# Who copies the transposed rows out of PSUM, and how row statistics are joined, in a macaron block on one core

## The reference

```
x = x + 0.5 * ffn(layernorm(x))
x = x + attn(layernorm(x))
x = x + 0.5 * ffn(layernorm(x))

# ffn: a mixture of experts, E = 16, width 128, and 2 shared experts
logits = x @ router_w.T ; scores = sigmoid(logits) ; s = scores + bias
# 4 groups of 4 experts; the 2 groups with the best top-2 sums; of them the top 4 experts
tw = scores of the four / their sum * 2.5
h = x @ gate_w[e] ; u = x @ up_w[e] ; y = (silu(h) * u) @ down_w[e]
routed = sum over e of y * weight[e] ; shared: silu(x @ sh_gate) * (x @ sh_up) @ sh_down
# attn: 32 heads of 4, no softmax, a group norm per head over all positions, output projection
```

## Time and profile before

| | |
|---|---|
| median of 3 runs | 740.83 us (739.88 to 741.75) |
| profiled execution, its own time | 739.06 us |
| its span in the trace | 737.3 us |
| PE busy | 677.0 us (92%) |
| DVE busy | 601.3 us (82%) |
| POOL busy | 433.6 us (59%) |
| ACT busy | 399.6 us (54%) |
| chain that ended last | PE 45%, DVE 28%, issue 15%, POOL 6%, ACT 3%, DMA 2% |

### The profile page before, as it was taken

The page is one execution under the profiler, slowest core; times in us unless marked ns, Lnnn a source line. Parts: engine busy times, 40 slices in busy tenths (PEclk is TensorE's granted clock), DMA queues, the critical chain, the costliest instruction groups (busy, mean ns, idle before and its releaser), DMA issues.

```text
span 737.3 us, 12023 instructions
## 1 busy us (share of the span) xinstructions
PE 677.0 (92%) x3116; PEld 539.6 (73%) x3116; DVE 601.3 (82%) x1571; ACT 399.6 (54%) x784; POOL 433.6 (59%) x373
## 2 busy tenths in 40 slices
PE   2497999999999998999988999889998999999997
PEld 2376878787877866678766787667776878787885
DVE  2889797969799797997978979879799797969664
ACT  2464556565666544656445564455654556565553
POOL 4565657575756645656555474554646657575664
PEclk9699999999999999999999999999999999999999
DMA  6550614060604105033060150500605014050600
GB/s 179 179 203 1 231 35 196 3 228 0 230 2 156 76 23 210 0 93 137 2 228 1 39 191 15 206 26 16 228 15 201 30 52 193 17 229 14 231 15 15
DMA packets 30789, 76.37 MB, mean 104 GB/s; under 512 B 3968, under 2 KB 12688, under 8 KB 30736
## 3 DMA queue, kind: packets, MB, share of 16 engines
q1 hardware_dynamic: 30736, 75.81, 28.7%
HBM read 73.18 MB, written 2.62 MB: 103 GB/s over the span
## 4 chain that ended last, share of the span: by engine, by line
PE 45%; DVE 28%; issue 15%; POOL 6%; ACT 3%; DMA 2%; DVEq 1%; POOLq 0%; SPq 0%; ACTq 0%
DVE T L961 9%; POOL A_lo L323 6%; PE gateP L413 6%; PE gateP L415 5%; PE gateP L414 5%; PE upP L413 4%; PE upP L415 4%; PE yP L413 4%; PE upP L414 4%; PE yP L415 4%; PE yP L414 4%; DVE A L983 3%; ACT gateP L664 1%; PE prepP L444 1%; DVE wsum L851 1%
## 5 line engine op out<-in xcount | busy, mean ns | idle before, releaser
L323 POOL TENSOR_TENSOR A_lo<-A,A_hi 128x512 fp32r<-128x512 f32 x288 | 372.6, 1300 | 197.1 <-ACT A_hi L681 196.6
L681 ACT CAST A_hi<-A 128x512 fp32r<-128x512 f32 x288 | 177.2, 615 | 121.6 <-DVE A L983 117.0
L664 ACT ACTIVATE gateP<-gateP 128x512 f32<-128x512 f32 x256 | 148.8, 581 | 137.9 <-PE gateP L415 136.4
L961 DVE TENSOR_TENSOR T<-gateP,CB 128x512 f32<-128x512 f32 x256 | 175.2, 684 | 55.2 <-ACT gateP L664 49.4
L983 DVE TENSOR_TENSOR A<-upP,T 128x512 f32<-128x512 f32 x256 | 177.0, 692 | 9.2
L413 PE MATMUL gateP<-XT_hi,W_hi 128*128 128x512 f32 x288 | 125.9, 437 | 17.5 <-DVE T L961 17.0
L413 PE MATMUL upP<-XT_hi,W_hi 128*128 128x512 f32 x288 | 115.1, 400 | 0.0
L415 PE MATMUL gateP<-XT_lo,W_hi 128*128 128x512 f32 x288 | 114.0, 396 | 0.0
L414 PE MATMUL gateP<-XT_hi,W_lo 128*128 128x512 f32 x288 | 113.6, 394 | 0.0
L415 PE MATMUL upP<-XT_lo,W_hi 128*128 128x512 f32 x288 | 113.6, 394 | 0.0
L413 PE MATMUL yP<-A_hi,W_hi 128*128 128x512 f32 x288 | 113.0, 392 | 0.6 <-POOL A_lo L323 0.6
(11 more groups left out here) (169 smaller groups left out, 677.6 us busy)
## 6 DMA issues: line engine op xcount, KB each, us to landing
CB<-combT SPq DMA_DIRECT2D x128, 512.0 KB, 6.2
out_dram<-X SPq DMA_DIRECT2D x8, 256.0 KB, 2.0
X<-in_L_attn_x_dram SPq DMA_DIRECT2D x3, 512.0 KB, 6.2
W_in<-in_L_ffn_gate_w_dram SPq DMA_DIRECT2D x4, 256.0 KB, 5.1
W_in<-in_L_ffn_up_w_dram SPq DMA_DIRECT2D x4, 256.0 KB, 5.1
W_in<-in_L_ffn_down_w_dram SPq DMA_DIRECT2D x4, 256.0 KB, 5.3
X<-in_L_attn_x_dram SPq DMA_DIRECT2D x2, 256.0 KB, 3.6
combT<-CT SPq DMA_DIRECT2D x16, 32.0 KB, 1.8
```

What stands on the lines that cost most here:

```text
L323: pool.tensor_tensor(A_lo[:, slot, :], A[:, slot, :], A_hi[:, slot, :].bitcast(F32), ALU.subtract).then_inc(low_done, 1)
L664: act.activation(dst, gateP[u % 2][:, :], ACT.Silu).then_inc(silu_done, 1)
L681: act.copy(A_hi[:, v % SLOTS, :], A[:, v % SLOTS, :]).then_inc(high_done, 1)
L961: dve.tensor_tensor(T[:, u % TS, :], gateP[u % 2][:, :], CB[:, e, :], ALU.mult).then_inc(gate_weighted, 1)
```

## The change

Three things are done together.

1. ACT reads `prepP` twice at w = 0, first with a cast to `XT_hi`, then as a plain copy to `XT`. DVE's copy (`next_full`) is gone, and so is the wait of ACT for it. `next_low` (POOL) and `logits` (PE) move from w = 1 to w = 2; the parts of `route` from w = 2 to 9 to w = 3 to 10; the transpose of the weights and their copy by ACT from w = 11 and 12 to 12 and 13; `route_silu` from w = 3 to 4. The residual stays at w = 7.
2. `bn_stats` moves from w = 12 to w = 11, and the seven operations behind it give way to four `bn_aggr`, one a tile, at w = 12 (`whole_stats`). In the places where attention work stands at u = 11 and u = 29, `bn_stats` comes ahead of it.
3. POOL adds epsilon and changes the sign of the mean, two operations of 128 x 4 ahead of the power.

```diff
-        parts = sb("parts", [P, 5, TILES])
+        mv = sb("mv", [P, TILES, 2])
+        eps_t = sb("eps_t", [P, TILES])
+        minus = sb("minus", [P, TILES])
...
             def step_rstd(t):
-                pool.wait_ge(stats_seq, 4 * (t + 1))
+                pool.wait_ge(stats_seq, 2 * (t + 1))
+                pool.tensor_tensor(vareps[:, :], mv[:, :, 1], eps_t[:, :], ALU.add).then_inc(rstd_ready, 1)
+                pool.tensor_tensor(nmean[:, :], mv[:, :, 0], minus[:, :], ALU.mult).then_inc(rstd_ready, 1)
+                pool.wait_ge(rstd_ready, 4 * t + 2)
                 pool.tensor_tensor(rstd[:, :], vareps[:, :], half[:, 0:TILES],
                                    ALU.pow).then_inc(rstd_ready, 1)
-                pool.wait_ge(rstd_ready, 2 * t + 1)
+                pool.wait_ge(rstd_ready, 4 * t + 3)
                 pool.tensor_tensor(shift[:, :], nmean[:, :], rstd[:, :], ALU.mult).then_inc(rstd_ready, 1)
             def next_low(t, q):
-                pool.wait_ge(xt_hi_ready, t + 1)
+                pool.wait_ge(xt_ready, t + 1)
...
-                    if w == (7 if early else 1) and not (last and s == 1):
+                    if w == (7 if early else 2) and not (last and s == 1):
                         next_low(2 * p + s + 1, (s + 1) % 2)
...
-                        if w == (7 if early else 1):
+                        if w == (7 if early else 2):
                             logits(t0 + s + 1)
-                        if w == (16 if early else 11):
+                        if w == (16 if early else 12):
                             transpose_weights(t0 + s + 1)
...
             def next_high(t, q):
-                act.wait_ge(xt_ready, t + 1)
-                act.copy(XT_hi[:, q, :], XT[:, :]).then_inc(xt_hi_ready, 1)
+                act.wait_ge(xt_done, t + 1)
+                act.copy(XT_hi[:, q, :], prepP[:, :])
+                if not (isinstance(t, int) and t == 0):
+                    act.wait_ge(xt_lo_ready, t)
+                act.copy(XT[:, :], prepP[:, :]).then_inc(xt_ready, 1)
...
-                        if w == (9 if early else 3):
+                        if w == (9 if early else 4):
                             route_silu(t0 + s + 1)
-                        if w == (17 if early else 12):
+                        if w == (17 if early else 13):
                             copy_weights(t0 + s + 1)
...
-                merge_stats(stats_seq, 4 * t, bst, nmean[:, :], vareps[:, :], parts)
-
-            def next_full(t):
-                dve.wait_ge(xt_done, t + 1)
-                if not (isinstance(t, int) and t == 0):
-                    dve.wait_ge(xt_lo_ready, t)
-                dve.tensor_copy(XT[:, :], prepP[:, :]).then_inc(xt_ready, 1)
+            def whole_stats():
+                for j in range(TILES):
+                    ins = dve.bn_aggr(mv[:, j, :], bst[:, j, :])
+                ins.then_inc(stats_seq, 1)
...
+                    if w == 12 and not last:
+                        dve.wait_ge(stats_seq, 2 * (t0 + s + 2) + 1)
...
                     if not (last and s == 1):
-                        at = 6 if early else 0
-                        if w == at:
-                            next_full(t0 + s + 1)
-                        if at + 2 <= w < at + 10:
-                            route(t0 + s + 1, w - at - 2)
+                        at = 8 if early else 3
+                        if at <= w < at + 8:
+                            route(t0 + s + 1, w - at)
                     if w == 12 and not last:
+                        whole_stats()
+                    if w == 11 and not last:
                         dve.wait_ge(mul_done, n + u + 1)
                         stats(t0 + s + 2, 2 * ((p + 1) % BATCH) + s)
```

More of the change, by code:

```diff
@@ L221, in macaron_kernel @@
         stats_seq, rstd_ready, xn_ready = sem("stats_seq"), sem("rstd_ready"), sem("xn_ready")
-        xt_done, xt_hi_ready, xt_lo_ready = sem("xt_done"), sem("xt_hi_ready"), sem("xt_lo_ready")
+        xt_done, xt_lo_ready = sem("xt_done"), sem("xt_lo_ready")
         xt_ready = sem("xt_ready")
@@ L599, in normalise @@
             def normalise(t, blk, part):
-                act.wait_ge(rstd_ready, 2 * (t + 1))
+                act.wait_ge(rstd_ready, 4 * (t + 1))
                 for j in range(part * TILES // 2, (part + 1) * TILES // 2):
@@ L968, in pair @@
                     early = first and s == 0
-                    if w in ((13, 14) if early else (7, 8)) and not (last and s == 1):
-                        dve.wait_ge(route_seq, ROUTE_OPS * (t0 + s + 1) + (21 if w in (7, 13) else 22))
+                    if w == 12 and not last:
+                        dve.wait_ge(stats_seq, 2 * (t0 + s + 2) + 1)
+                    if w in ((13, 14) if early else (8, 9)) and not (last and s == 1):
+                        dve.wait_ge(route_seq, ROUTE_OPS * (t0 + s + 1) + (21 if w in (8, 13) else 22))
                     dve.wait_ge(silu_done, n + u + 1)
@@ L989, in pair @@
                         stats(1, 1)
+                        dve.wait_ge(stats_seq, 3)
+                        whole_stats()
                     if not (last and s == 1):
-                        at = 6 if early else 0
-                        if w == at:
-                            next_full(t0 + s + 1)
-                        if at + 2 <= w < at + 10:
-                            route(t0 + s + 1, w - at - 2)
+                        at = 8 if early else 3
+                        if at <= w < at + 8:
+                            route(t0 + s + 1, w - at)
                     if w == 12 and not last:
+                        whole_stats()
+                    if w == 11 and not last:
                         dve.wait_ge(mul_done, n + u + 1)
@@ L1003, in pair @@
                         attention_stage(u, p - ATT0)
+            dve.memset(eps_t[:, :], EPS)
+            dve.memset(minus[:, :], -1.0)
             dve.memset(comb[:, :], 0.0)
@@ L1007, in _ @@
             stats(0, 0)
-            next_full(0)
+            dve.wait_ge(stats_seq, 1)
+            whole_stats()
             dve.wait_ge(router_in, 32)
             dve.wait_ge(const_seq, CONSTS)
-            dve.wait_ge(xt_hi_ready, 1)
+            dve.wait_ge(xt_ready, 1)
             dve.tensor_tensor(XT_lo[:, 0, :], XT[:, :], XT_hi[:, 0, :].bitcast(F32),
```

## The result

The changed kernel takes **754.13 us** (median of 6 runs, 752.33 to 756.85); the kernel before took 740.03 on the same chip (6 runs). The ratio is 1.0189, 95% interval 1.0173 to 1.0205. The forecast was 731.0, with a range from 724.5 to 739: wrong in sign. The profiled span grew from 737.3 to 751.5.

A forecast was written before the change was run, and what follows sets the result against it. PE was taken to bound plain steps, with gains only from its idle time in attention steps and step 0. Terms -3.6 - 6.0 + 0 + 0.7 - 1.0 + 0.1 = -9.8 off median 740.83 gave 731.0 us, range 724.5 to 739.

The forecast's parts named there:

- signs of being right: No logits wait at loop heads, w = 7 gate matmul on time, first attention steps near 45, second 47.2, plain 39.7 to 39.9.
- signs of being wrong: Second attention steps above 49, ACT's Silu waiting behind both copies, `bn_aggr` as long as `bn_stats`, or the w = 7 stall remaining.
- Plain steps: Steps 1, 2, 3, 12, 13: old stall stays, DVE slightly overfull at w = 11; +0.13 each, +0.7 in all.
- port rule: A DVE operation with two SBUF inputs shares a port with GpSimd; whichever starts first holds it for the whole instruction.
- rival B: Second attention steps: `wsel`, `wsum + 1e-20` and `comb` each blocked by an `A_lo`; +4 a step, total 747; chance 0.09.
- Second attention steps: Steps 5, 7, 9, 11: +0.9 `bn_stats`, +1.1 one routing block, -2.0 two operations freed; 0, between -1 and +3 each.
- Loop heads: Steps 6, 8, 10: PE's wait for `XT` shrinks, 1.1 saved plus 0.1 for a restart; -1.2 each, -3.6 in all.
- w = 3 to 16 of first attention steps: Steps 4, 6, 8, 10: stalls at w = 7 and 15 go, `s_row` comes late; -1.5 each, -6.0 in all.
- Step 0 and start: Step 0: `comb` 1.0 earlier, PE's wait 2.94 to 1.9, -1.0; start: logits 0.4 later, +0.1.
- Prices: Costs of added work: four `bn_aggr` about 0.4 a step; ACT's copies and POOL's two operations nothing.

## Why the prediction was wrong

The step that failed is the move of the routing by one unit, which the prediction put at nothing in the plain steps and at the loop heads and at a gain in the second attention steps; it costs 27.7. Of the 24 us between the forecast and the profile 7.5 lie in the plain steps, 9.2 behind the loop heads and 6.3 in the second attention steps. Its signs of being right name the length of a plain step (39.7 to 39.9; it is 41.0), none of its signs of being wrong does.

- *Plain steps*, forecast +0.7 in all, bounds -1 to +4: **+8.2**. It read "one unit later the same string begins and ends one unit later, so this stall stays". The string is not the same: w = 7 holds the residual, ahead of the routing part, and part 4, with its two-input `masked`, came to stand behind it and beside POOL's `A_lo`, 1.36 instead of 0.22. I costed the removed and added work of w = 11 and never laid the moved parts beside what stood in their new units. Both views were there: the order of the instructions and POOL's `A_lo`, one in every unit. And I had put the port rule in front of rival B only, for the attention steps, though `A_lo` runs in plain steps as well.
- *Second attention steps*, forecast 0: **+6.3** in all. Rival B had one of the two mechanisms, `wsum` and `comb` held up by the pile, and PE's wait for `comb` is 1.51 there; the other is `masked` again, 1.59 at w = 10. I gave rival B 0.09 and +4 a step; measured were +1.6, with the statistics moving the other way: with them alone at the old places these steps fell by 1.35.
- *Loop heads*, forecast -1.2 a head and with the -1.5 of the next point -2.7 a step: steps 6, 8 and 10 came out **+0.3** each. The wait for `XT` went as said, and with the copies alone it was worth 1.7 a head, more than my 1.2. But I took the 3 us on issue for a constant. They follow the DMA traffic, and the edit moved the traffic. Behind the wait of 1.86 at 298.95 the granted clock was 0.60 (298.95 to 304.00), mostly 1.2 GHz; with DVE unrolled, without the wait, it was 1.00 in the same place. But the clock is not what the step lost: behind the head of step 8 PE waited longer, 2.02, and had 1.00, and that step takes 48.2 against 48.3 and 48.4 of steps 6 and 10. Step 8 has later waits instead (0.94 at w = 7, 0.53 for `comb`, 0.46 for `s_row`), which step 6 does not have. The table by stretch of the changed kernel behind the heads of steps 6 and 8:

```profile
298.95:304.00 5.05, 5.04 (x18) 4.36 (x19) 4.86 (x17) 1.72 (x3) 3.74 (x3) 0.60 0.00 0
396.01:401.06 5.05, 4.87 (x25) 4.16 (x26) 4.86 (x17) 3.02 (x6) 3.79 (x3) 1.00 0.00 0
```

and of the changed kernel with DVE unrolled:

```profile
299.00:304.00 5.00, 5.00 (x25) 4.19 (x25) 4.76 (x17) 3.28 (x8) 4.09 (x5) 1.00 0.00 0
```

- *w = 3 to 16 of first attention steps*, forecast -1.5 each: step 4, which has no head, gained **1.3**. Right in size there, and mostly for the reasons given: the waits of 1.44 at w = 7 and 0.52 at w = 15 are gone, the one for `s_row` is 0.44 instead of the 1.0 put in; a wait of 0.54 for `comb` came on top. In step 8 the one at w = 7 is still 0.94.
- *Step 0 and start*, forecast -0.9: **0**, but traces of the same code differ there by up to 1.4, so one trace of each kernel could not show it. But PE's wait for `comb`, which was to fall from 2.94 to 1.9, is 3.42, and it is 3.42 with copies and aggregate at the old places too: `comb` did not come earlier against PE.
- *Prices*: four `bn_aggr` 0.37 (forecast 0.4); ACT's copies hidden; POOL's two operations hidden. Right. The sum of the costed parts, about -10, is what the edit would have given without the move (-14.2 measured), though not place by place. The +0.7 put in for the plain steps was for `bn_stats` at w = 11, not for the move.

## What to carry to other kernels

When a string of operations moves by a unit, lay each of them beside what the other engines and its own queue do in the new unit; a DVE operation with two SBUF inputs that begins just behind a long GpSimd one can stand until that one ends (1.36 instead of 0.22 us here), and the order of two neighbours can decide it (17.6 us in all here). Split an edit of several parts before judging it: two good parts were hidden by one bad one. And look at a loop's head for "issue" time: a hot engine's loop may be cheaper written out (11.0 us in the kernel before, on one engine alone).

## What the runs showed of the hardware that was not expected

- The jump back of a loop of 425 to 439 DVE instructions leaves DVE idle for 3.0 to 3.2 us, with one instruction packet of 8 KB, which begins 2.0 to 2.1 us before the first operation (the same operation is 0.77 behind DVE's last one where the loop is written out, changed kernel). With the DMA engines 93% busy it is 4.5 to 4.6; with the loop's beginning four instructions ahead of place 512, 4.2 to 4.4 and two packets.
- Two operations that want the same port within 0.01 us go one way or the other from step to step of one run, 0.23 or 1.36 us for the same `masked`.
- What PE's lower clock costs depends on where it falls. With the residual behind part 4, 3.4 us at 1.2 GHz cost steps 5 and 11 1.6 us in w = 14 and 15. In step 9 the same 3.4 us lay in w = 13 (granted clock 0.63 there, step 7 has 1.00) and cost nothing: PE's wait for `zb` behind them was 0.26 instead of 1.57, and steps 7 and 9 are equally long.
